# Even/odd spectral part, statistics-based layer norm and reordered stage ends in a two-stage convolution kernel

## The reference

```python
def _gn(v, G=32, eps=1e-05):   # 32 groups of one channel: mean and variance of each image's channel
    ...
x = x + _L0_conv_ref(_gn(x), ...)      # dynamic depthwise 3x3, then a 1x1 mix
x = x + _L1_conv_ref(_gn(x), ..., 8)   # spectral product on 8x8 patches, gated by v
```

```python
hidden = jnp.einsum('oc,bchw->bohw', w_hidden, x)            # 32 -> 192 channels
hidden = depthwise 3x3 of hidden
q, k, v = jnp.split(hidden, 3, axis=1)                       # 64 channels each
out = irfft2(rfft2(patches(q)) * rfft2(patches(k)))          # on 8x8 patches
out_norm = layer norm of out over its 64 channels, per pixel
return jnp.einsum('oc,bchw->bohw', w_out, v * out_norm)
```

## Time and profile before

| what | value |
|---|---|
| median of 3 runs | 2920.11 us |
| profiled execution | 2927.13 us, span 2925.3 us |
| mean granted TensorE clock | 0.962 |
| PE busy | 2646.9 us (90%) |
| ACT busy | 2148.9 us (73%) |
| DVE busy | 1946.4 us (67%) |
| POOL busy | 562.0 us (19%) |
| DMA | 248.07 MB, 85 GB/s over the span |

### The profile page before, as it was taken

The page is one execution under the profiler, slowest core; times in us unless marked ns, Lnnn a source line. Parts: engine busy times, 40 slices in busy tenths (PEclk is TensorE's granted clock), DMA queues, the critical chain, the costliest instruction groups (busy, mean ns, idle before and its releaser), DMA issues.

```text
span 2925.3 us, 85696 instructions
## 1 busy us (share of the span) xinstructions
PE 2646.9 (90%) x34055; PEld 1709.4 (58%) x34055; DVE 1946.4 (67%) x3320; ACT 2148.9 (73%) x4429; POOL 562.0 (19%) x325
## 2 busy tenths in 40 slices
PE   6888888499999999999999999999999999999998
PEld 3333333266666666666666666666666666666664
DVE  5566665467676767676766666666676767666676
ACT  3555555478787878787878787878787878787885
POOL 1000000112222222222222222222222222222222
PEclk9889988799999999999999999999999999999999
DMA  6687876712222222222222222222222222222211
GB/s 122 164 216 209 219 213 166 190 32 60 61 60 61 60 61 60 61 60 61 60 61 63 59 64 57 68 54 68 57 67 58 66 55 67 57 65 56 66 43 44
DMA packets 60343, 248.07 MB, mean 85 GB/s; under 512 B 12393, under 2 KB 12658, under 8 KB 53714
## 3 DMA queue, kind: packets, MB, share of 16 engines
q1 hardware_dynamic: 59954, 242.47, 34.0%
HBM read 140.71 MB, written 101.72 MB: 83 GB/s over the span
## 4 chain that ended last, share of the span: by engine, by line
PE 74%; DVE 13%; issue 7%; ACT 5%; DMA 1%; SPq 0%; DVEq 0%; ACTq 0%; POOL 0%
PE bank L575 15%; PE bank L657 14%; PE bank L516 13%; PE bank L637 8%; PE bank L588 6%; PE bank L648 6%; PE bank L560 6%; PE bank L597 4%; DVE arena L1085 3%; ACT arena L841 3%; DVE arena L1105 2%; DVE arena L1169 2%; DVE arena L1099 1%; DVE arena L1078 1%; PE bank L530 1%
## 5 line engine op out<-in xcount | busy, mean ns | idle before, releaser
L841 ACT ACTIVATE arena<-bank 64x256 f32<-64x256 f32 x2048 | 773.2, 378 | 144.4 <-PE bank L648 125.9
L444 POOL TENSOR_TENSOR arena<-arena 128x8 f32<-128x8 f32 x256 | 515.0, 2012 | 1848.9 <-DVE arena L1107 1848.7
L575 PE MATMUL bank<-arena 128*64 128x512 f16 x4608 | 717.0, 402 | 45.1 <-issue 45.1
L784 ACT ACTIVATE arena<-bank 100x512 f32<-100x512 f32 x1024 | 583.7, 635 | 122.1 <-PE bank L560 119.9
L1169 DVE TENSOR_TENSOR arena<-bank,arena 128x512 f32<-128x512 f32 x512 | 354.4, 692 | 460.2 <-ACT arena L841 401.0
L657 PE MATMUL bank<-arena 100*128 100x128 f32 x4096 | 592.8, 288 | 0.0
L657 PEld LDWEIGHTS bank<-arena 100*128 100x128 f32 x4096 | 498.3, 192 | 82.9 <-issue 82.7
L560 PEld LDWEIGHTS bank<-arena 128*64 128x64 f16 (+1 forms) x8192 | 343.1, 107 | 280.3 <-issue 49.8
L560 PE MATMUL bank<-arena 128*64 128x128 f16 (+1 forms) x8192 | 416.7, 225 | 48.3 <-DVE arena L1078 28.8
L516 PE MATMUL bank<-arena 32*32 32x508 f32 (+1 forms) x9216 | 393.2, 669 | 70.4 <-issue 35.9
L800 ACT ACTIVATE arena<-bank,arena 128x256 f32<-128x256 f32 x512 | 261.4, 561 | 139.4 <-PE bank L588 136.6
(11 more groups left out here) (116 smaller groups left out, 1901.6 us busy)
## 6 DMA issues: line engine op xcount, KB each, us to landing
arena<-xn_d SPq DMA_DIRECT2D x128, 536.2 KB, 8.3
xn_d<-arena SPq DMA_DIRECT2D x130, 260.0 KB, 5.0
x_d<-arena SPq DMA_DIRECT2D x64, 512.0 KB, 8.1
arena<-x_d SPq DMA_DIRECT2D x128, 256.0 KB, 4.7
out<-arena SPq DMA_DIRECT2D x128, 256.0 KB, 4.3
arena<-x_in SPq DMA_DIRECT2D x32, 544.0 KB, 9.9
arena<-x_in SPq DMA_DIRECT2D x32, 528.0 KB, 9.8
arena<-spectra_in SPq DMA_DIRECT2D x1, 1152.0 KB
```

The lines of the kernel that those rows point to most:

```text
L444: pool.tensor_tensor(tiny["rstd"][:, slot], tiny["var_eps"][:, slot], powers, ALU.pow).then_inc(s_root, 1)
L575: mm = pe.matmul(v_banks[chunk % 3][64 * s:64 * s + 64, :], v_w[:, 64 * tap:64 * tap + 64], at(xs[half], row * WP + 32 * k + dx, [32 * WP, ...
L784: act.activation(h_rows[0:WIN, :, first:first + 4], banks[g % ring][0:WIN, :].rearrange("p (i c) -> p c i", i=4), ACT.Copy).then_inc(s_h_r ...
L841: ins = act.activation(at(q_sb[n % 4][64 * to:64 * to + 64, :], 128 * half, [256, 2], [1, 128]), src, ACT.Copy)
```

## The change

In stage 2:
- Channels are handled in pairs, even and odd. The k transforms of a pair give the two parts (real and imaginary) separately: 64-column weights, the even channel on partitions 0 to 63 and the odd one on 64 to 127. q is not doubled any more: one ACT copy of a whole bank for eight channels (an octet), and the product reads it by broadcast for both parts. The inverse contracts over 64 partitions twice and accumulates; its weights stand on both partition halves, its results go to two banks, by the parity of the channel.
- k has three banks instead of two, and `prod` two buffers of an octet. The inverse of an octet follows the first k group of the next octet. Chunk 0 of v of the same unit stands before the last inverse.
- The layer norm begins when all of Y is there. BATCH_NORM_STATS on two neighbouring pixels, interleaved, gives mean and variance for both (its even and odd halves); ACT's squares and the channel sums are gone, and the slots for the roots are four deep.
- PE's front has two hidden groups, chunk 1 with four, then the first turn; the other groups are spread over the later chunks.

In stage 1: `xh` and `xl` exist once; the small matmuls from pooled on are at steps 9, 11, 13 and 15; DVE's and ACT's pieces are reordered around them; the loop ends at the last image, and the norm, high and low parts of the last two images are done beside the hidden groups of unit 0; the arena is laid out so that the first windows can be loaded before stage 1 ends; the memset of `hwin` is gone (all spectral matmuls read 100 rows). At the start the weight preparation on DVE is 10 broadcast instructions instead of 40, POOL's memsets of `xh` and `xl` wait for it, and the taps' matmuls no longer wait for v's weights.

```diff
-            for b in range(-1, NB + 1):
+            pe.wait_ge(s_low_parts, 1)
+            for b in range(-1, NB):
...
+                if chunk == 0:
+                    pe.wait_ge(s_prod_ready, 16 * u + 14)
+                if chunk in (1, 2):
+                    pe.wait_ge(s_y_ready, 8 * (u + 1) - 2 + chunk)
...
-                v_chunk(tail, v_half, 0, 0, 6, hidden)
-                v_chunk(tail, v_half, 0, 1, 6, hidden)
-                turn(tail, 0, 0)
+                hidden(2)
+                for k in range(4):
+                    v_chunk(tail, v_half, k, 1, (4, 5, 4, 3)[k], hidden)
...
+                def k_quad(n, octet=None):
+                    if positive(16 * u + n - 2):
+                        pe.wait_ge(s_prod_ready, 16 * u + n - 2)
...
+                    for pair in range(2):
+                        for part in range(2):
+                            if octet is not None and pair == 1 and part == 1:
+                                inverse_inputs(octet)
+                            for par in range(2):
+                                ch = 4 * n + 2 * pair + par
+                                mm = pe.matmul(k_banks[n % 3][64 * par:64 * par + 64, 256 * part + 128 * pair:256 * part + 128 * pair + 128],
+                                               G_k[0:WIN, 128 * ch + 64 * part:128 * ch + 64 * part + 64],
+                                               hwin[0:WIN, 128 * (64 + ch):128 * (64 + ch) + 128], start=True, stop=True)
...
+                def inverse_octet(m):
+                    for part in range(2):
+                        for par in range(2):
+                            for lam in range(2):
+                                mm = pe.matmul(i_banks[par][64 * lam:64 * lam + 64, 256 * (m % 2):256 * (m % 2) + 256],
+                                               small["inverse"][64 * par:64 * par + 64, 64 * part:64 * part + 64],
+                                               at(prod[m % 2][64 * par:64 * par + 64, :], 256 * part + 64 * lam, [512, 2], [128, 2], [1, 64]),
+                                               start=part == 0, stop=part == 1)
...
+                for m in range(8):
+                    if m < 7:
+                        q_octet(m + 1)
+                    if m == 0:
+                        k_quad(0)
+                    else:
+                        k_quad(2 * m, m - 1)
+                        inverse_octet(m - 1)
+                    k_quad(2 * m + 1)
...
+                v_chunk(u, half, 0, 0, 0, None, lambda: inverse_inputs(7))
+                inverse_octet(7)
...
+            def pixel_stats(u, p):
+                if p == 0:
+                    dve.wait_ge(s_y_ready, 8 * (u + 1))
+                for s in range(2):
+                    for j in range(0, 4, 2):
+                        first = 24 * (p % 4) + 12 * s + 3 * j
+                        ins = dve.bn_stats(T["pixel_stats"][:, first:first + 6], at(Y, 2048 * s + 4 * p + j, [32, 64], [1, 2]))
...
+                for p in range(3):
+                    pixel_stats(tail, p)
+                    variance(tail, p)
+                    if p == 1:
+                        centre(tail, 0)
+                scale(tail, 0)
```

More of the change, by code:

```diff
@@ L58, in constants @@
     a = 2 * np.pi * ((u[:, None] * u[None, :] + v[:, None] * v[None, :]) % 8) / 8
-    out["inverse"] = (np.concatenate([np.cos(a) + np.sin(a), np.sin(a) - np.cos(a)]) / 64).astype(np.float32)
+    both = np.concatenate([np.cos(a) + np.sin(a), np.sin(a) - np.cos(a)], axis=1) / 64
+    out["inverse"] = np.tile(both, (2, 1)).astype(np.float32)
     return out
@@ L103, in build @@
         s_pads_stored = semaphore("pads_stored")
-        s_xn_out = [semaphore(f"xn_out{s}") for s in range(2)]
+        s_xn_out = semaphore("xn_out")
         s_transforms_in = semaphore("transforms_in")
@@ L243, in build @@
         x2 = [x2_0, x2_1, x2_2]
-        hilo = [[take(QPIX // W * WP, f16) for _ in range(2)] for _ in range(2)]
-        xh, xl = [[hilo[1 - s][part] for s in range(2)] for part in range(2)]
+        xh, xl = [take(QPIX // W * WP, f16) for _ in range(2)]
         prep_qk, prep_v = x2[1][:, 0:128], x2[1][:, 128:128 + 9 * 128]
@@ L277, in build @@
             ("v_max", 1), ("v_inv", 1), ("d_max", 1), ("d_inv", 1), ("v_back", 1), ("dw_qk_s", 9), ("dw_v_n", 9))}
+        stage1_end = top[0]
+        top[0] = phases
+        hwin = take(128 * 128)
+        Y = take(64 * 64)
+        q_sb = [take(512) for _ in range(2)]
+        prod = [take(1024) for _ in range(2)]
+        gated = [take(512) for _ in range(2)]
+        res = take(2048)
+        xs_1, xs_0 = [take(HALF * WP, f16) for _ in range(2)]
+        xs = [xs_0, xs_1]
+        assert stage1_end <= top[0] - (HALF * WP + 1) // 2
+        G_q = take(64 * 64)
+        G_k = take(64 * 128)
+        win = [take(1632, f16) for _ in range(2)]
         block = ctx.enter_context(nc.Block())
@@ L414, in _ @@
                 pool.wait_ge(s_x_edges, 2 * s + 2)
-            for s in range(2):
-                pool.memset(xh[s].bitcast(f32), 0.0).then_inc(s_pads_zero, 1)
-                pool.memset(xl[s].bitcast(f32), 0.0).then_inc(s_pads_zero, 1)
+            pool.wait_ge(s_prep_v, 1)
+            pool.memset(xh.bitcast(f32), 0.0).then_inc(s_pads_zero, 1)
+            pool.memset(xl.bitcast(f32), 0.0).then_inc(s_pads_zero, 1)
             for s in range(2):
@@ L571, in v_chunk @@
                 for tap in range(9):
+                    if tap == 8 and before_last is not None:
+                        before_last()
                     dy, dx = tap // 3, tap % 3
@@ L661, in spectral @@
+                q_octet(0)
+                if tail is not None:
+                    turn(tail, 3, 1)
+                for m in range(8):
[3 more added lines that the diff above has]
+                        k_quad(0)
+                    else:
+                        k_quad(2 * m, m - 1)
+                        inverse_octet(m - 1)
+                    k_quad(2 * m + 1)
+                    if m == 0 and tail is not None:
                         project(tail, 3)
-                    if n > 0:
-                        inverse(n - 1)
@@ L757, in _ @@
                         evacuate(here, k)
+                gate_exp(after)
                 centre_x(after, 2)
                 centre_x(after, 3)
-                gate_exp(after)
-                norm(prev, 0)
                 if b < 0:
@@ L812, in front @@
                 if tail is None:
-                    some(32)
-                    return
-                some(4)
-                square(tail, 0)
-                some(1)
-                square(tail, 1)
-                some(4)
-                square(tail, 2)
-                for p, groups_before in enumerate((3, 4, 4, 3, 3, 3, 3)):
+                    some(8)
+                    high(NB - 2, 0)
+                    high(NB - 2, 1)
+                    some(8)
+                    norm(NB - 1, 0)
+                    norm(NB - 1, 1)
+                    some(16)
+                    high(NB - 1, 0)
+                    high(NB - 1, 1)
+                    act.wait_ge(s_xl_ready, 4 * NB)
+                    return
+                for p, groups_before in enumerate((6, 5, 5, 5, 4, 4, 3)):
                     some(groups_before)
                     turned_out(tail, p // 2, p % 2)
-                    if p + 3 < 8:
-                        square(tail, p + 3)
                 if u is None:
@@ L1109, in scale @@
+                dve.tensor_tensor(piece, piece, over(T["pixel_mean"][:, 8 * (p % 4):8 * (p % 4) + 8]), ALU.subtract).then_inc(s_y_centred, 1)
             def scale(u, p):
```

364 lines of the change are left out of this document (161 added, 203 removed).

## The result

The changed kernel takes 2888.9 us (median of 4 runs, 2878.7 to 2896.0) against 2919.3 (4 runs): ratio 0.9889, 95% interval 0.9856 to 0.9922. It is faster by some 30 us, or 1.1%, where 182 us were forecast, and outside the predicted range of 2655 to 2815. The profiled execution has a span of 2887.8 us, 37.5 less than before.

| stretch | forecast | measured |
|---|---|---|
| start to the convolution's end (539.4, now 516.4) | -29 | -23.0 |
| from there to the end of unit 0's last inverse | -17 | -13.8 |
| units 1 to 31 | -140 | +2.6 |
| the last front | -3 | -3.2 |

A forecast was written before the change was run, and what follows sets the result against it. Stage 2 was taken as PE-bound; savings of 140 (units), 4, 3 (last front), 24 (images), 13 (between stages) and 5 (start) sum to 189 us, from 2927.1 to 2738, range 2655 to 2815.

The forecast's parts named there:

- the forecast for the units (-140): Stage 2's half-image units: each 4.5 us shorter, from spectral savings of 5.2 and front waits, times 31.
- Octet 3.8 us: Spectral part on PE: two groups of four channels take 3.8 us instead of 4.22, saving 3.3 us a unit.
- A: Rival: row halves take turns in the inverse, 1.96 us an octet, +251 us, total 2989; chance 0.04.
- D: Rival: k gains nothing at half width, octet stays 4.22 us, +105 us, total 2843; chance 0.06.
- E: Rival: fewer block changes and no lost clock, octet 3.55 us, -64 us, total 2674; chance 0.20.
- Spectral part: Spectral part of a stage 2 unit on PE: all its savings together, -5.2 us a unit.
- Statistics 0.21 us apart: Layer norm on DVE: 32 statistics instructions of 128 elements start 0.21 us apart, 6.7 us a unit.
- rival B: DVE becomes the front's bound, statistics instructions at 0.30 us each, +75 us, total 2813; chance 0.14.
- First turn: Stage 2 front: first turn possible 6.1 us after the last inverse, PE waiting 2.5 us in one parity.
- Images -24: First stage: small matmuls 2 to 3 steps earlier make weights ready before an image ends, 1.5 us each, 16 times.
- Rival C: First-stage ends give nothing, other PE idle time or the single xh taking it back; total 2778; chance 0.15.
- Between the stages: Convolution's end to DVE's first product: 42 us instead of 55.4, a gain of 13 (8 to 18).

The follow-up runs named there:

- e1: Changed kernel with DVE's window copies r = 4 to 7 moved ahead of the gate of their iteration; 2753.3 us, ratio 0.9455 to the kernel before.
- e4: Changed kernel with PE's hidden groups spread as 2, then 6, 4, 4, 4, 4, 4, 4 by chunk, DVE's order kept; 2728.2 us, ratio 0.9374.
- e2: Changed kernel with only half of the statistics instructions (16 of 32 a unit); 2853.6 us, ratio 0.9802 to the kernel before.
- e3: Changed kernel with the first piece scaled before the third's statistics and variance; 2873.8 us, ratio 0.9854 to the kernel before.
- e6: Kernel of e5 with the first piece also scaled before the third's statistics; 2729.6 us, ratio 0.9367 to the kernel before.
- e9: Kernel of e4 with the first stage's four small products back on steps 11, 13, 15, 18; 2744.6 us, ratio 0.9411 to the kernel before.
- e7: Changed kernel without the middle of nine taps of the v convolution; 2902.4 us, ratio 0.9954 to the kernel before.
- e5: Changed kernel with window copies ahead of the gate (r = 3 too) and hidden groups spread evenly; 2723.7 us, ratio 0.9343 to the kernel before.

## Why the prediction was wrong

The step that failed is the one on the front: "Afterwards DVE needs per piece 0.9 + 0.3 + 3 x 0.69 + a third for residual and half a window: 3.9 us, PE per chunk [...] 4.2. PE stays the bound, barely". Each amount in it is about right (DVE's add up to 3.8), and the conclusion doesn't follow. I summed what each engine does in a turn's time, and took the largest sum. The chain that runs through all three (turn, ACT's copy, gate, centring, scaling, residual, window copy, hidden group, turn) is 5.5 us, longer than any sum. All its links were in the change, though not all in the parts of the diff shown above: DVE's `windows()` moved from ahead of the gate to the end of the iteration, and PE's groups, 12 ahead of the first turn before and 6 now, were spread so that three of them stood last ahead of a turn with a new window to wait for. That is 127 us of PE's waits, and 140 us by e1; with the circle cut, the forecast for the units (-140) is met by e1's stage 2 (2283.9 - 2143.3 = 140.6) and passed by e4's (158.8). That it is met within a us is luck in part: single terms were off by some 0.5 us a unit, as the points below show.

The other points:
- *Octet 3.8 us*: right, 3.80, but partly by luck. Block by block it is k 0.98, inverse 1.03, k 0.92, q 0.87, so against the earlier trace rows k gave 2 x 1.08 - 1.90 = 0.26, q 1.08 - 0.87 = 0.21, and the inverse took 0.05 more. The four changes of block at 0.1 each are not what the trace shows. Where the tile shape stays (100*64 for both k and q), the next block starts 0.17 us before the modelled end of the last one (1303.90 + 1.09 - 1304.82 and 1304.82 + 1.04 - 1305.69; from inverse to q in the earlier trace rows too). Where the shape changes, it is 0.06 to 0.08 us (1302.87 + 1.10 - 1303.90 and 1305.69 + 1.04 - 1306.67; q to k and k to inverse in the earlier trace rows). So a change of shape costs 0.1 us more than one of block alone; an octet has two of them where it had four, some 0.2 of the 0.42 gained. The other 0.2 of my 0.4 is that the blocks themselves take more than 0.053 us an instruction. The Trainium skill (TensorEngine Tiling (Array Packing), Key Properties) has the engine drain when the tiling mode changes, not just the tile. The trace agrees, with 0.1 us for it; so the rule spoke for this change, not against it as the prediction has it. Rivals A, D and E fall.
- *Spectral part*: first q to the end of the last inverse took 1354.88 - 1317.68 = 37.2 us before; it takes 1396.01 - 1361.13 = 34.9 with a v chunk of 2.2 in it. Like for like -4.6 against -5.2.
- *Statistics 0.21 us apart*: right, 0.20; rival B's price of 0.30 is not seen, and e2 shows that the statistics set nothing in the changed kernel outside the first turn. The Trainium skill (SBUF — State Buffer, the note on cachelines in Door 1) has no penalty where a line is hit twice; the 0.20 us are in keeping with that, and no run here reads the same tile with one hit a line.
- *First turn*: forecast at +6.1 us after the last inverse with 2.5 of waiting, measured 1401.72 - 1396.01 = +5.7 and 1.84. The other parity waits nothing, as forecast. That an earlier turn would be worth its wait is true only in part (e3 -10 to -18 us, e6 nothing).
- *Images -24*: measured -19.7, mechanism as stated (e9). Rival C falls.
- *Between the stages*: first product 45.2 us after the convolution's end (561.65 - 516.4), forecast 42, before 55.4. The wait is named as forecast, the store that must land:
```profile
561.65 1.29 DVE L1197 TENSOR_TENSOR arena<-bank,arena 128x512 f32<-128x512 f32 x2 [10.33 <-DMA xn_d<-arena]
```
- *Start -5*: measured 53.98 - 50.71 = -3.3. The weights are ready near 9.5 us, as forecast, and the loads win, the last of them that of the small table `tap_rows`:
```profile
20.92 1.99 PE L466 MATMUL bank<-arena 9*96 9x512 f32 x2 [10.24 <-DMA arena<-tap_rows_in]
```

I named the sign that came: "Wrong it is [...] if stage 2 does not shrink by 100 us or more"; the one beside it, "if PE waits for DVE in every chunk", came for three chunks of a unit. The rival behind it was drawn as an amount of work (B), not as an order.

## What to carry to other kernels

Where engines work in turns, sum the chain from an event to its next occurrence through all engines, beside the work of each engine; the longest of them was the period here (5.5 us against 4.2). For every instruction that a diff moves behind a waiting one, ask who needs its result and whether that one stands ahead of what the wait is for: if so, a circle is closed, and work taken off an engine beside the circle left its waits as they were (e2) or lengthened them (e7). Two waits on the same circle are cured by one cut (e1, e4, e5), and both cuts here are a matter of order, with no instruction changed.

## What was not expected of the hardware

Less work on PE made a kernel slower: with one tap in nine left out the mean granted clock was 0.948 to 0.952 in all eight runs against 0.965 to 0.967 in the four with all taps, and the time 2902.4 against 2888.9 us. A period set by other engines gives PE its savings as gaps. What a lower clock costs is seen from two units of the changed kernel, from last inverse to last inverse, with the same work at a mean clock of 1.00 and of 0.98:
```profile
814.28:885.40 71.12, 64.76 (x961) 44.79 (x960) 41.43 (x100) 35.75 (x64) 14.07 (x8) 1.00 0.26 62
958.60:1031.31 72.71, 66.35 (x960) 45.67 (x960) 41.41 (x100) 35.84 (x64) 13.74 (x8) 0.98 0.25 61
```
PE is busy 1.59 us more in the second, and the unit is 1.59 us longer. A unit of the kernel with the tap left out:
```profile
957.48:1030.24 72.76, 64.78 (x945) 45.09 (x944) 41.41 (x100) 35.09 (x64) 13.74 (x8) 0.98 0.25 61
```
It has less work, and PE is as long at it as the changed kernel at full clock: part of the saving went into slower matmuls and not into waits, which is why the waits grew by 17 us only. An estimate for the whole: the clock has two levels, 1.2 and 2.4 GHz, so the means of the profiled executions say (1 - 0.950) x 2 x 2903.9 = 290 us at the lower one against (1 - 0.967) x 2 x 2887.8 = 191. A hundred us more at half the clock cost up to 50 us of PE's time; a front of the kernel without the tap gains 0.56 us from its first turn to its seventh (1359.63 - 1330.14 = 29.49 against 1360.49 - 1330.44 = 30.05), 17 us over 31 units. So the clock is large enough to turn the gain into the loss of 16 us between the two spans. No run changed the clock alone, and which gaps lowered it was not tried.
